# Segment and chunk sums as pairs of fp16 products, and new orders of work on ScalarE and VectorE in the decode stages

## What is computed

```python
proj = u @ W_in.T                       # z, x, B, C, dt
xBC = silu(causal_conv1d(xBC, conv_w) + conv_b)
A = -exp(A_log); dt = softplus(dt + dt_bias); dA = exp(dt * A)
S = S * dA[t] + dt[t] * outer(B[t], x[t]); y[t] = S @ C[t]     # 8 heads of 64
y = (y + D_param * x) * silu(z) ; out = y @ W_out.T
x = u + layernorm(out)
x = x + layernorm((silu(n @ Wg.T) * (n @ Wu.T)) @ Wd.T)        # n = layernorm(x)
```

## Time and profile before

| | us |
|---|---|
| median of 3 runs | 1444.87 (1444.31 to 1446.34) |
| the profiled execution's own time | 1443.4 |
| its span | 1441.7 |
| PE busy | 1361.3 (94%) |
| DVE busy | 933.8 (65%) |
| ACT busy | 577.1 (40%) |
| POOL busy | 457.6 (32%) |

### The profile page before, as it was taken

How to read it: one execution, slowest core, us unless ns; L and a number is a source line. 1 busy time by engine, 2 the same in 40 slices (tenths; PEclk the granted TensorE clock), 3 DMA queues, 4 the chain that set the end, 5 groups by cost and what they waited for, 6 DMA issues and landing times. The chain is left out here.

```text
span 1441.7 us, 19103 instructions
## 1 busy us (share of the span) xinstructions
PE 1361.3 (94%) x6912; PEld 672.6 (47%) x6912; DVE 933.8 (65%) x1869; ACT 577.1 (40%) x1018; POOL 457.6 (32%) x691
## 2 busy tenths in 40 slices
PE   4878987988999999999999999999999999999998
PEld 2334444444554445444545445544554444444443
DVE  7978866987577656765676567755775555544432
ACT  5466655676444234332434243423442233122120
POOL 1312233333233434334322433254334242310102
PEclk9889998999999999999999999999999999999999
DMA  5133233322310223013301320032102110311201
GB/s 164 37 102 88 69 93 100 92 75 56 74 45 23 59 70 85 19 36 93 73 16 52 88 71 26 23 92 77 44 23 71 39 44 23 97 43 30 74 1 51
DMA packets 99021, 87.79 MB, mean 61 GB/s; under 512 B 68208, under 2 KB 68208, under 8 KB 98928
## 3 DMA queue, kind: packets, MB, share of 16 engines
q1 hardware_dynamic: 97040, 86.54, 21.8%
q10 hardware_dynamic: 1888, 0.03, 0.1%
HBM read 54.05 MB, written 16.78 MB: 49 GB/s over the span
## 5 line engine op out<-in xcount | busy, mean ns | idle before, releaser
L1312 PE MATMUL bank<-fxt,ffn_hi 128*128 128x512 f16 (+1 forms) x1408 | 418.8, 379 | 2.0 <-DVE dn L1677 1.5
L1312 PE MATMUL bank<-fxt,ffn_lo 128*128 128x512 f16 (+1 forms) x704 | 266.8, 379 | 0.0
L1312 PEld LDWEIGHTS bank<-fxt,ffn_hi 128*128 128x128 f16 (+1 forms) x1408 | 139.8, 100 | 173.1 <-issue 12.9
L1210 PE MATMUL bank<-mask,diag 128*128 128x416 f16 x640 | 128.0, 354 | 21.7 <-ACT ffn_lo L830 20.2
L605 POOL TENSOR_TENSOR state<-state,ex 64x512 f32<-64x512 f32 x32 | 36.8, 1149 | 343.3 <-PE bank L1265 342.3
L1326 PE MATMUL bank<-ffn_hi,h_hi 128*128 128x512 f16 (+1 forms) x352 | 133.5, 379 | 0.0
L1326 PE MATMUL bank<-ffn_hi,h_lo 128*128 128x512 f16 (+1 forms) x352 | 133.4, 379 | 0.0
L1326 PE MATMUL bank<-ffn_lo,h_hi 128*128 128x512 f16 (+1 forms) x352 | 133.3, 379 | 0.0
L1643 DVE SCALAR_TENSOR_TENSOR gact<-gact,bank 128x512 f32<-128x512 f32 (+1 forms) x88 | 60.2, 684 | 105.7 <-ACT gact L874 104.8
L874 ACT ACTIVATE gact<-bank,c_gate_half 128x512 f32<-128x512 f32 (+1 forms) x88 | 59.9, 681 | 154.7 <-PE bank L1312 153.1
L1496 DVE TENSOR_SCALAR mask<-codes_h 128x832 f16<-128x832 f16 x320 | 111.7, 408 | 12.5 <-PE bank L1210 12.2
(11 more groups left out here) (184 smaller groups left out, 2357.3 us busy)
## 6 DMA issues: line engine op xcount, KB each, us to landing
codes_sb<-codes SPq DMA_DIRECT2D x80, 208.0 KB, 3.4
ures<-u SPq DMA_DIRECT2D x32, 256.0 KB, 2.8
x_scratch<-x SPq DMA_DIRECT2D x32, 256.0 KB, 2.0
ut<-x_scratch SPq DMA_DIRECT2D x16, 512.0 KB, 4.3
xres<-x_scratch SPq DMA_DIRECT2D x32, 256.0 KB, 3.0
out<-dn SPq DMA_DIRECT2D x32, 256.0 KB, 2.1
ut<-u SPq DMA_DIRECT2D x15, 512.0 KB, 4.4
ffn_hi<-w_in_t SPq DMA_DIRECT2D x4, 580.0 KB, 9.2
```

The lines of the kernel that those rows point to most:

```text
L1210: last = nc.tensor.matmul(p.bank[:, 0:COLS], diag[:, q].rearrange("p n m -> p (n m)"), mask[:, n, q, j * COLS:(j + 1) * COLS], start=(q == ...
L1312: last = nc.tensor.matmul(bank, wt[:, c0:c0 + w], fxt[:, :, half, k, :], start=(k == 0 and n == 0), stop=(k == KC - 1 and n == 2))
```

## The change

1. da becomes two fp16 pieces, scaled by 256 (a_sb is multiplied by -256, and the product is held above -60000); the exponentials on ACT take the scale 1/256. In DVE's time_steps this is three instructions of 128x32 more.
2. The chunk sums are six fp16 products (three matrices, two pieces) in place of three fp32 products; the segment sums are four fp16 products in place of two fp32 ones. causal, below and ones exist in fp16, made once at the start.
3. POOL writes both terms for the segment sums, two products of 128x1024 with fp16 inputs and output, into the bytes of decay, in place of one in fp32.
4. In the decode stages ACT and DVE have a list of their own, decode_stage. The FFN stages keep the order they had. SP, POOL and PE keep theirs.

```diff
-                    seg_ready.inc(nc.gpsimd.tensor_tensor(
-                        decay[:], causal[:].unsqueeze(1).broadcast_to((P, HEADS, P)),
-                        da[:, t % HALVES, c, :].unsqueeze(2).broadcast_to((P, HEADS, P)), ALU.mult))
+                    for n in range(2):
+                        seg_ready.inc(nc.gpsimd.tensor_tensor(
+                            segs[:, n], causal_h[:].unsqueeze(1).broadcast_to((P, HEADS, P)),
+                            da[:, t % HALVES, c, n, :].unsqueeze(2).broadcast_to((P, HEADS, P)), ALU.mult))
...
-                    for n, sums in enumerate((causal, below, ones)):
-                        last = nc.tensor.matmul(p.bank[:, 192 + n * HEADS:192 + (n + 1) * HEADS], sums[:],
-                                                da[:, half, c, :], start=True, stop=True)
+                    for n, sums in enumerate((causal_h, below_h, ones_h)):
+                        for piece in range(2):
+                            last = nc.tensor.matmul(p.bank[:, 192 + n * HEADS:192 + (n + 1) * HEADS], sums[:],
+                                                    da[:, half, c, piece, :], start=(piece == 0), stop=(piece == 1))
...
                     for n in range(2):
-                        last = nc.tensor.matmul(seg_banks[n][:], below[:],
-                                                decay[:, 4 * n:4 * n + 4, :].rearrange("p h t -> p (h t)"),
-                                                start=True, stop=True)
+                        for piece in range(2):
+                            last = nc.tensor.matmul(seg_banks[n][:], below_h[:],
+                                                    segs[:, piece, 4 * n:4 * n + 4, :].rearrange("p h t -> p (h t)"),
+                                                    start=(piece == 0), stop=(piece == 1))
...
                     chain(dt_steps, i, 17, nc.vector.tensor_tensor(
-                        da[:, p], dt[:], a_sb[:].unsqueeze(1).broadcast_to((P, SUB, HEADS)), ALU.mult))
+                        dtp[:], dt[:], a_sb[:].unsqueeze(1).broadcast_to((P, SUB, HEADS)), ALU.mult))
+                    chain(dt_steps, i, 18, nc.vector.tensor_scalar(dtp[:], dtp[:], SEG_LOW, None, ALU.max))
+                    chain(dt_steps, i, 19, nc.vector.tensor_copy(da[:, p, :, 0, :], dtp[:]))
+                    chain(dt_steps, i, 20, nc.vector.tensor_sub(da[:, p, :, 1, :], dtp[:], da[:, p, :, 0, :]))
```

The new list of ACT in stages 0 and 1, first half (before, codes_to_half(k + 4) opened the stage, each further one came one decoded earlier, and the two slices of the second u pair stood at the same place, ahead of decoded(t, 3)):

```diff
+                    decoded(t, 0)
+                    codes_to_half(k + 4)
+                    small(t, 1)
+                    decays(t, 1)
...
+                    normalise_slice("u", t + 1, 0, 0)
+                    normalise_slice("u", t + 1, 0, 1)
+                    decoded(t, 1)
+                    y_transposed(t, 0)
+                    codes_to_half(k + 5)
+                    decoded(t, 2)
+                    out_projected(t, 0)
+                    codes_to_half(k + 6)
+                    normalise_slice("u", t + 1, 1, 0)
+                    normalise_slice("u", t + 1, 1, 1)
+                    decoded(t, 3)
+                    codes_to_half(k + 7)
+                    decoded(t, 4)
+
+                    decoded(t, 5)
+                    codes_to_half(k + 8)
+                    dt_input(t + 1)
+                    conv_input(t + 1, 4)
```

More of the change, by code:

```diff
@@ L906, in stage @@
-                    if dec:
-                        normalise_slice("u", t + 1, 0, 0)
-                        normalise_slice("u", t + 1, 0, 1)
-                        decoded(t, 1)
-                        codes_to_half(k + 6)
-                    if ffn:
-                        gate_tanh(g, 2)
+                    high(g, 1)
+                    normalise(t - 1, 3)
+                    gate_tanh(g, 2)
                     y_transposed(t, 0)
-                    if ffn and nxt:
+                    if nxt:
@@ L927, in stage @@
[L927 to L939 removed]
+                    high(g, 2)
+                    gate_tanh(g, 3)
@@ L1010, in stage @@
                         conv_input(t + 1, 3)
-                    if dec:
-                        decoded(t, 12)
-                        codes_to_half(k + 17)
-                    if ffn:
-                        high(g, 10)
+                    high(g, 10)
                     out_projected(t, 2)
@@ L1050, in stage @@
                     out_projected(t, 3)
-                    if dec:
-                        decoded(t, 18)
-                        codes_to_half(k + 23)
                     if nxt:
@@ L1127, in _ @@
                 codes_to_half(3)
-                for t in range(TILES):
+                for t in range(LAG):
+                    decode_stage(t)
+                for t in range(LAG, TILES):
                     stage(t)
@@ L1692, in stage @@
                     y_gated(t, 0)
-                    if ffn:
-                        times_up(g, 0)
-                    y_split(t, 0, k + 2 if dec else None)
-                    if ffn and nxt:
+                    y_split(t, 0, k + 2)
+                    weigh(t, 1)
+                    decayed(t, 1)
+                    masks(k + 3)
+                    if t == 0:
+                        out_weights_low()
+                    ln_split("u", t + 1, 0, 0)
+                    ln_split("u", t + 1, 0, 1)
@@ new lines, in decode_stage @@
+                    masks(k + 4)
+                    ln_stats("u", t + 1, 1)
+                    masks(k + 5)
+                    ln_split("u", t + 1, 1, 0)
+                    ln_split("u", t + 1, 1, 1)
+                    masks(k + 6)
+                    y_sum(t, 1)
+                    out_stats(t, 0)
+                    y_gated(t, 1)
+                    y_split(t, 1, k + 7)
+                    dt_input(t + 1)
+                    weigh(t, 2)
+                    conv(t + 1, 4)
+                    decayed(t, 2)
@@ new lines, in decode_stage @@
+                    masks(k + 8)
+                    conv_silu(t + 1, 4)
+                    if ffn_next:
+                        ln_stats("x", t - 1, 0)
+                    masks(k + 9)
+                    conv(t + 1, 0)
+                    time_steps(t + 1)
+                    masks(k + 10)
+                    conv_silu(t + 1, 0)
+                    masks(k + 11)
+                    if t % HALVES == 1:
+                        clear_state((t + 1) // HALVES)
+                    y_sum(t, 2)
@@ new lines, in decode_stage @@
+                    out_stats(t, 1)
+                    y_gated(t, 2)
+                    y_split(t, 2, k + 12)
+                    conv(t + 1, 1)
+                    weigh(t, 3)
+                    decayed(t, 3)
+                    masks(k + 13)
+                    conv_silu(t + 1, 1)
+                    conv(t + 1, 2)
+                    masks(k + 14)
+                    conv_silu(t + 1, 2)
+                    conv(t + 1, 3)
+                    masks(k + 15)
+                    conv_silu(t + 1, 3)
@@ new lines, in decode_stage @@
+                    if ffn_next:
+                        ln_split("x", t - 1, 0, 0)
+                        ln_split("x", t - 1, 0, 1)
+                    masks(k + 16)
+                    y_sum(t, 3)
+                    out_stats(t, 2)
+                    z_gate(t + 1, 0)
+                    y_gated(t, 3)
+                    y_split(t, 3, k + 17)
+                    weigh(t + 1, 0)
+                    decayed(t + 1, 0)
+                    masks(k + 18)
+                    if ffn_next:
+                        ln_stats("x", t - 1, 1)
@@ new lines, in decode_stage, with stage @@
+                    masks(k + 19)
+                    z_gate(t + 1, 1)
+                    masks(k + 20)
+                    if ffn_next:
+                        ln_split("x", t - 1, 1, 0)
+                        ln_split("x", t - 1, 1, 1)
+                    ln_stats("u", t + 2, 0)
+                    z_gate(t + 1, 2)
+                    z_gate(t + 1, 3)
+                    masks(k + 21)
+                def stage(t):
+                    g = t - LAG
+                    nxt = t + 1 < TILES
+                    y_sum(t, 0)
+                    out_stats(t - 1, 3)
+                    gate_silu(g, 0)
+                    y_gated(t, 0)
+                    times_up(g, 0)
+                    y_split(t, 0)
+                    if nxt:
@@ L1729, in stage @@
[L1729 to L1733 removed]
+                    gate_silu(g, 3)
+                    low(g, 2)
+                    times_up(g, 3)
+                    gate_silu(g, 4)
+                    low(g, 3)
+                    times_up(g, 4)
                     y_sum(t, 1)
                     out_stats(t, 0)
[L1737 to L1738 removed]
+                    low(g, 4)
```

390 lines of the change are left out of this document (160 added, 230 removed).

## The result

The changed kernel takes **1461.8 us** (median of 4 runs, 1459.1 to 1464.3), the kernel before 1445.2 on the same chip: ratio 1.0122, 95% interval 1.0096 to 1.0148. It is 1.2% slower, where I had forecast 1423 us, faster, with a range that ended at 1440. The profiled span is 1460.4 us.

A forecast was written before the change was run, and what follows sets the result against it. PE bounds the FFN stages; in the decode stages it waits on other engines. FFN -23.4, decode +0.6, prologue +0.9 give -21.9 from 1443.4, so 1421.5, and 1423 us with the median's 1.5 us offset; range 1402 to 1440.

The forecast's parts named there:

- PE's part: Chunk and segment sums on PE: 1.45 us saved per step, 33.4 us over 23 steps of the FFN stages.
- The new wait for gact: FFN stages, second half of gate_up(g, 7): DVE's gact late, PE waits 2.0 us in five stages, 10 us in all.
- The hold of the transpose: Decode stages: SP issues u's second transpose only after codes_to_half(k+8), now behind decoded(t, 5); project_dt 8.3 us later.
- The fourth quarter: Decode stages, last quarter: waits for yt and ffn_lo go, z projection wait stays; -3.5 us, between -6 and 0.
- my three signs of being wrong: POOL's fp16 products take 1 us; no PE wait in FFN stages; project_dt still starts 7.2 us after the scan.
- the second quarter: Decode stages, y_sum(1) to y_sum(2): the held transpose delays project_dt and is not won back, +8.3 us per stage.
- decode 5 ends at S + 6.9: First link of the second quarter's chain: PE's decode(t, 5) ends 6.9 us after the scan's start S.
- I count nothing for it: PE's granted clock after waits in decode stages: two waits go, one comes in each stage, so 0 us.
- the chain of u ends where it did: Decode stages, first quarter: next tile's u chain, then decoded(t, 3), sets its end; 0 us, between -4 and +2.
- the third quarter: Decode stages: conv_tanh(2) behind conv_input(3) removes PE's 2.78 us wait for cin; -4.5 us, between -6 and 0.
- rival 1: Decode stages: transposes not held, ACT reaches codes_to_half(k+8) early enough or DVE is late anyway; 1406 us, chance 0.22.
- Rival (3): POOL/DVE lock at every step: each FFN step loses 0.45 us, decode stages 17 us; 1472 us, chance 0.05.

The follow-up runs named there:

- e8: Changed kernel with 30 unused fp16 products on PE ahead of its wait for the transposed xt: 1455.8 us, ratio 1.0102.
- e1: Kernel before with only the fp16 sums and POOL's two products, old ACT and DVE decode orders: 1435.2 us, ratio 0.9932.
- e18: Changed kernel with only ACT's conv_input(t+1, 2) moved ahead of conv_tanh(t+1, 1): 1446.9 us, ratio 1.0032.
- e13: Changed kernel, ACT's codes_to_half(k+8) ahead of decoded(t, 5), u's second-pair slices behind decoded(t, 3), conv_input(t+1, 2) ahead of conv_tanh(t+1, 1): 1420.3 us, ratio 0.9838.
- e5: e1 with POOL writing only the first segment product and PE multiplying it twice: 1425.0 us, ratio 0.9865.
- e10: e1 plus DVE's new decode-stage order, ACT's order as before: 1448.4 us, ratio 1.0034.
- e2: Kernel before with only the new ACT and DVE decode orders, fp32 sums and one POOL product: 1471.3 us, ratio 1.0192.
- e9: e1 plus ACT's new decode-stage order, DVE's order as before: 1466.8 us, ratio 1.0145.
- e14: e1 with gate_silu(g, 6) and conv_input(t+1, 2) moved early, plus the first quarter of e13's ACT decode list: 1425.5 us, ratio 0.9870.
- e16: e1 with gate_silu(g, 6), conv_input(t+1, 2) and y_transposed 0, 1, 3 moved early, the last ahead of codes_to_half: 1423.5 us, ratio 0.9868.

## Why the prediction was wrong

**Right.** PE's part: 1.45 us per step, as summed; 23 steps. POOL's product at 1.9 us, hidden from PE in the FFN stages. The new wait for gact, in the half and for the reason named, though not by the sizes named: low takes 1.74 us for 0.66 (forecast +1.2), the taps 2.99 for 2.33 (forecast up to +1.8), out_rstd ends 1.1 us later and not 1.9, since POOL had idled there, and the half waits 1.51 us where I took 2.0. Laid over the saving of 1.45, the steps c = 1 lost 8.8 us in five stages where I had 10, and the steps c = 0, which wait for gact too, another 4.2 (0.63 in four stages, 1.66 in t = 6), which I did not have. So the FFN stages gave 20.4 us for 23.4. The prologue: +1.5 against +0.9. The hold of the transpose, with its cause in SP's order. The fourth quarter as a small gain (2.1 and 5.4 us from y_sum to y_sum, 3.5 forecast). The first is off by little: 0 forecast; in stage 0 it is 6.3 us longer but begins 4.5 sooner, in stage 1 it is 1.3 longer. None of my three signs of being wrong came: they tested the terms that were right.

**Wrong, the second quarter: +8.3 forecast, +19.1 and +17.9 measured** from y_sum(1) to y_sum(2). The step that failed is its first line, "decode 5 ends at S + 6.9". It was read from a scan at 2.4 GHz. In the changed kernel the scan and the first part of decode 5 run at 1.2 GHz and end at S + 11.4; from there my steps hold (to xt 8.3 us, forecast 8.6), so project_dt starts at S + 19.6 and not at S + 15.5 (S + 19.3 in stage 1). And what followed the wait I had at full clock too: convolution 4 lost 2.5 us, and 1.2 in stage 1. DVE shows this as idle time, 18.9 us in this quarter of stage 0 where it was 2.7. The third piece is in its busy time, 4.1 us more than before: the last row is eight masks, 2.36 us by themselves, beside POOL's state product and its two segment products.

```profile
112.77 0.69 DVE L1625 TENSOR_TENSOR y<-y,bank 128x512 f32<-128x512 f32 x1 [2.98 <-PE bank L1291]
...
128.47 0.19 DVE L1567 TENSOR_TENSOR dtx<-dtr,dt_bias_sb 128x32 f32<-128x32 f32 x1 [6.46 <-ACT dtr L806]
...
136.61 0.55 DVE L1603 TENSOR_TENSOR gram<-gram,causal 128x128 f32<-128x128 f32 x1 [7.50 <-ACT gram L855]
...
155.22 6.62 DVE L1518 TENSOR_SCALAR mask<-codes_h 128x832 f16<-128x832 f16 x8
```

2.98 us for the slow scan, 6.46 for dtr behind the held transpose, 7.50 for gram behind the slow convolution (before, the first of these waits was 0.46 us and the longest of the quarter 1.21). Of the 37 us by which the decode stages missed the forecast, 20.4 lie in this quarter of the two stages and 16.4 in the third.

**Wrong, the clock: "I count nothing for it".** I had counted waits, two gone and one come in each stage, and not asked where they stand. The waits that went stood ahead of decode and project_out; the ones that came stand ahead of the scan and of the convolution on which DVE's y and xs hang. e8 prices the second such place at 1 to 2.5 us a stage; at the first, the scan and decode 5 took 11.4 us for 6.9. And the 4.67 and 4.95 us that left the first quarter were not gone but gathered: 8.68 us at one point, and 5.16 for ysplit besides. My sentence that the chain of u ends where it did was right, and its consequence, one long wait directly ahead of the scan, I did not draw.

**Wrong, the third quarter: -4.5 forecast, +2.0 and +5.4 measured.** I wrote that conv_tanh(2) behind conv_input(3) removes the wait for cin. It removes one of two obstacles. The other, conv_tanh(1) ahead of conv_input(2), is the same in both orders. The wait grew from 2.78 to 5.0 us in e1, where DVE is not late, and to 7.49 in the changed kernel, where y_sum(2) is 10 us behind the scan. e18 and e13 price it at 13 to 16 us; it is the second cause of the loss.

**Wrong, POOL in the decode stages: nothing counted.** I weighed the second product in the FFN stages only. e1 is 9 us longer in the decode part than before; one product less takes 4.4 of it back. Of DVE's instructions there the second product stretches above all one, the addition of xd in y_gated (0.68 us, 1.87 beside POOL): 5.1 us more in e1's decode part than before, nothing more in e5's. I had looked for such stalls on instructions with two inputs in SBUF; the masks, one input, fp16, stand still beside POOL as well (6.62 for 2.36 us), and they are the largest group of DVE on the page, 123.8 us, all of it before 402 us. The Trainium skill has this (SBUF — State Buffer, "Who interferes with whom"): tensor_scalar, too, can take the shared ports in its fast modes; the trace agrees with the 6.62. But what brought them beside POOL is ACT's order and not the second product: they take 111.7 us before, 110.9 in e1 and 113.0 in e10, and 122.8 in e2 (one product, both orders) and 124.8 in e9. Where the other 5 us of e1 are, no run here settles.

The gains that I gave ACT's order elsewhere (rival 1 rested on them) do not exist: e14 and e16 take away waits of 4.7 us and gain nothing, in e14 since DVE comes no sooner, in e16 since PE then waits for the next bank. The sum by measured terms: -20.4 + 37.7 + 1.5 = +18.8 in place of -21.9. Rival (3) had the sign, but it took the loss in the FFN stages, where there is none, and only 17 us in the decode stages.

## What to carry to other kernels

When a change moves waits about in a stage with waits of some microseconds, price where each new wait stands: what runs behind it can run at half clock, as the scan and decode 5 did here (11.4 us for 6.9), and a chain worked out from a trace at full clock is then too short. Before an in-order engine (ACT here) waits for a second engine, it should have taken what a third has ready: conv_input(2) ahead of conv_tanh(1) was worth some 15 us in the changed kernel and took one line. A freed wait is a gain only where the next engine is not as late: read the other engine's lag behind the scan before and expect the wait to come back there.

## What of the hardware was not expected

DVE's fp16 mask instructions, one input and one output in SBUF, stop beside POOL's: eight of them 6.62 us in place of 2.36, with 5.1 us of POOL under them. POOL's product takes 1.89 us in the median with fp16 inputs and output, as with fp32. And with PE kept busy by products for nothing during a wait of 8 us, the convolution behind took 2.6 us in place of 5.1 in stage 0, and in place of 3.8 in stage 1.
